# Short-tile combination on GpSimd and strip copy on VectorE in an attention and mixture-of-experts block

## What is computed

```python
q, k, v = x @ wq.T, x @ wk.T, x @ wv.T          # 8 heads, 2 maps of 32, v of 32
scores = einsum('bhqd,bhkd->bhqk', q, k) / sqrt(dh)      # 16 maps, causal
attn = softmax(scores + causal, axis=-1)
attn = attn[:, :8] - attn[:, 8:] * lmbda                 # the two maps of a head
out = einsum('bhqk,bhkd->bhqd', attn, v)
o = out * rsqrt(mean(out ** 2 over groups of 4) + eps) * (1 - L_INIT)
x = x + (o @ wo.T) * silu(ffn(layernorm(x)))
```

## Time and profile before

| | us |
|---|---|
| median of 3 runs | 1129.12 (1128.27 to 1133.16) |
| the profiled execution | 1129.73 |
| its span | 1127.9 |

### The profile page before, as it was taken

How to read it: one execution, slowest core, us unless ns; L and a number is a source line. 1 busy time by engine, 2 the same in 40 slices (tenths; PEclk the granted TensorE clock), 3 DMA queues, 4 the chain that set the end, 5 groups by cost and what they waited for, 6 DMA issues and landing times. The chain is left out here.

```text
span 1127.9 us, 25764 instructions
## 1 busy us (share of the span) xinstructions
PE 945.8 (84%) x6626; PEld 662.2 (59%) x6627; DVE 937.6 (83%) x1873; ACT 776.0 (69%) x1982; POOL 222.6 (20%) x427
## 2 busy tenths in 40 slices
PE   5889875899999899898998988967999999963665
PEld 4777653666666666666666666644555555532544
DVE  6677667999999999999999999954777777754886
ACT  3544245999999999999999999962333333325563
POOL 2000000132222222222222222220000000017771
PEclk9999985999999999999999999998999999986677
DMA  7999965768777686775756657401222222223563
GB/s 260 353 359 335 330 258 146 160 163 202 171 173 165 158 204 170 178 160 117 165 128 137 155 119 166 99 20 59 79 80 84 79 79 83 79 92 95 168 184 104
DMA packets 92410, 178.11 MB, mean 158 GB/s; under 512 B 11744, under 2 KB 50144, under 8 KB 91360
## 3 DMA queue, kind: packets, MB, share of 16 engines
q1 hardware_dynamic: 74336, 147.38, 48.9%
q0 software_dynamic: 7680, 20.98, 6.5%
q10 hardware_dynamic: 10368, 9.44, 2.5%
HBM read 108.56 MB, written 69.21 MB: 158 GB/s over the span
## 5 line engine op out<-in xcount | busy, mean ns | idle before, releaser
L1049 DVE TENSOR_REDUCE nmax<-bank 128x1 f32<-128x1024 f32 (+3 forms) x256 | 259.8, 1015 | 4.2 <-PE bank L881 4.1
L982 ACT ACTIVATE Pr_long<-bank,nmax 128x1024 f32<-128x1024 f32 (+3 forms) x256 | 252.1, 985 | 11.0 <-DVE nmax L1049 10.8
L1009 ACT COPY AT<-bank 128x512 f32<-128x512 f32 (+3 forms) x384 | 177.1, 493 | 3.8 <-PE bank L920 1.8
L879 PE MATMUL bank<-Ks_first,Qs_first 128*128 128x512 f32 (+3 forms) x384 | 124.2, 413 | 31.1 <-ACT Pr_short L996 19.8
L996 ACT ACTIVATE Pr_short<-bank,nmax 128x128 f32<-128x128 f32 (+3 forms) x256 | 138.4, 541 | 8.9 <-DVE nmax L1067 1.7
L1241 PE MATMUL bank<-gu_sb,xsT 128*128 x288 | 139.8, 609 | 4.7 <-DVE hid L1358 0.5
L920 PE MATMUL bank<-ident,Pr_long 128*128 128x128 f32 x832 | 127.4, 280 | 18.1 <-DVE Pr_long L1099 18.0
L1099 DVE SCALAR_TENSOR_TENSOR Pr_long<-Pr_long,coef 128x1024 f32<-128x1024 f32 (+3 forms) x128 | 137.3, 1073 | 0.0
L879 PE MATMUL bank<-Ks_second,Qs_second 128*128 128x512 f32 (+3 forms) x384 | 119.4, 400 | 18.4 <-ACT Pr_short L996 18.1
L881 PE MATMUL bank<-maskb,identb 128*128 128x128 bf16 x512 | 118.1, 233 | 0.0
L920 PEld LDWEIGHTS bank<-ident,Pr_long 128*128 128x128 f32 x832 | 90.4, 142 | 31.4 <-issue 27.3
(11 more groups left out here) (147 smaller groups left out, 1634.5 us busy)
## 6 DMA issues: line engine op xcount, KB each, us to landing
q_parts<-PARTS SPq DMA_DIRECT2D x32, 512.0 KB, 5.1
k_parts<-PARTS SPq DMA_DIRECT2D x32, 512.0 KB, 3.7
Qs_first<-q_parts SPq DMA_DIRECT2D x64, 256.0 KB
Ks_first<-k_parts SPq DMA_DIRECT2D x64, 256.0 KB
Qs_second<-q_parts SPq DMA_DIRECT2D x64, 256.0 KB, 6.1
Ks_second<-k_parts SPq DMA_DIRECT2D x64, 256.0 KB, 7.0
xs_dram<-zeros SPq DMA_DIRECT2D x8, 1152.0 KB, 7.4
xs<-xs_dram SPq DMA_DIRECT2D x72, 128.0 KB, 2.0
```

The lines of the kernel that those rows point to most:

```text
L879: nc.tensor.matmul(at[:, c0:c1], Qs[head][:, m, q * P:(q + 1) * P], Ks[head][:, m, c0:c1], start=True, stop=(c1 < N))
L982: nc.scalar.activation(long_probs(p)[:, m, 0:N], long_slot[m][:, 0:N], ACT.Exp, bias=nmax[:, 4 * p + m:4 * p + m + 1], scale=1.0, accum_ou ...
L1009: nc.scalar.copy(AT[u % 6][:, 0:w], tb[u % BANKS][:, 0:w]).then_inc(unit_out, 1)
L1049: nc.vector.tensor_reduce(nmax[:, 4 * p + m:4 * p + m + 1], long_slot[m][:, 0:N], AX.X, ALU.max, negate=True).then_inc(long_maxed, 1)
```

## The change

`combine_short` moves from VectorE to GpSimd, where it is two instructions: the second map is scaled in place by `coef`, and behind a wait on its own semaphore (`short_scaled`) it is added to the first. `out_rows` moves from ScalarE to VectorE, with the last copy behind the loop. The frames of all engines are written anew; GpSimd's program is now run by `run_pairs` with a lead of four, with the two copies of V as steps of pairs 1 and `NP` - 3. The diff, without its semaphore declarations:

```diff
             short_slot = bank[2][:, 0:CH]
@@ -801,6 +803,22 @@
                         for u in range(2):
                             load(it + 1, u)
 
+                def combine_short(it, p):
+
+                    if absent(it, p):
+                        return
+                    it, p = place(it, p)
+                    N = (short_q(p) + 1) * P
+                    probs = short_probs(p)
+                    nc.gpsimd.wait_ge(coef_done, credited(it, NP, p))
+
+                    nc.gpsimd.sem_inc(combine_begun, 1)
+                    nc.gpsimd.tensor_scalar(probs[:, 1, 0:N], probs[:, 1, 0:N], coef[:, 2 * p:2 * p + 1], None, ALU.mult
+                                            ).then_inc(short_scaled, 1)
+                    nc.gpsimd.wait_ge(short_scaled, credited(it, NP, p))
+                    nc.gpsimd.tensor_tensor(probs[:, 0, 0:N], probs[:, 1, 0:N], probs[:, 0, 0:N], ALU.add
+                                            ).then_inc(short_combined, 1)
+
                 @block.gpsimd
                 def _(pool):
                     pool.sem_inc(vj_ready, 2)
@@ -850,26 +868,33 @@
                         nc.gpsimd.tensor_copy(d1_all[:, bass.ds(it * 2 + u, 1), :],
                                               dsum[u][:, :, 0].unsqueeze(1)).then_inc(d1_kept, 1)
 
-                    def iteration(it):
-                        for p in range(NP):
+                    def frame(it, p):
+                        if p >= 0:
                             if p == 0:
                                 for u in range(2):
-                                    copy_v(it, u)
                                     load_rows(it, u)
                             keep_rows(it, p)
-                            if p in SORT_AT:
-                                sort_rows(it, *SORT_AT[p])
-                            if p == 2:
-                                keep_d1(it, 0)
-                        keep_d1(it, 1)
-                        for u in range(2):
-
-                            pool.wait_ge(rows_sorted[u], 32 * (it + 1))
+                            if p == 1 and not (isinstance(it, int) and it == 0):
+                                copy_v(it, 1)
+                            if p == NP - 3 and not (isinstance(it, int) and it == NIT - 1):
+                                copy_v(it + 1, 0)
+                        combine_short(it, p + 4)
+                        if p in SORT_AT:
+                            sort_rows(it, *SORT_AT[p])
+                        if p == 2:
+                            keep_d1(it, 0)
+                        if p == NP - 1:
+                            keep_d1(it, 1)
+                            for u in range(2):
+
+                                pool.wait_ge(rows_sorted[u], 32 * (it + 1))
 
                     pool.sem_inc(o_kept, NP)
-                    iteration(0)
-                    with pool.Fori(1, NIT) as it:
-                        iteration(it)
+                    pool.sem_inc(short_combined, NP)
+                    pool.sem_inc(short_scaled, NP)
+                    for u in range(2):
+                        copy_v(0, u)
+                    run_pairs(pool, 4, frame)
                     keep_rows(NIT - 1, NP)
 
                 def score_into(at, head, q, m):
@@ -954,16 +979,16 @@
                     pe.sem_inc(pv_done, NP)
 
                     def frame(it, p):
+                        score_short(it, p + 2, 1)
+                        score_long(it, p + 3, 0)
+                        turn(it, p, LONG1)
                         turn(it, p + 1, LONG0)
                         score_short(it, p + 3, 0)
                         score_long(it, p + 3, 1)
                         turn(it, p + 1, SHORT)
                         values(it, p)
-                        score_short(it, p + 3, 1)
-                        score_long(it, p + 4, 0)
-                        turn(it, p + 1, LONG1)
-
-                    run_pairs(pe, 4, frame)
+
+                    run_pairs(pe, 3, frame)
                     pe.wait_ge(o_out, credited(NIT - 1, NP, NP - 1))
                     sum_rows(NP - 1).then_inc(pv_done, 1)
 
@@ -1008,36 +1033,22 @@
                     w = len(unit_blocks(p, k)) * P
                     nc.scalar.copy(AT[u % 6][:, 0:w], tb[u % BANKS][:, 0:w]).then_inc(unit_out, 1)
 
-                def out_rows(it, p):
-
-                    if absent(it, p):
-                        return
-                    it, p = place(it, p)
-                    nc.scalar.wait_ge(pv_done, credited(it, NP, p))
-                    nc.scalar.wait_ge(o_kept, credited(it, NP, p - 2))
-                    nc.scalar.copy(Ob[p % 2][:], ob[:, 0:P + 2 * DH]).then_inc(o_out, 1)
-
                 @block.scalar
                 def _(act):
                     act.sem_inc(long_exped, 2 * NP)
                     act.sem_inc(short_exped, 2 * NP)
                     act.sem_inc(unit_out, UNITS)
-                    act.sem_inc(o_out, NP)
 
                     def frame(it, p):
-                        exp_long(it, p + 3, 1)
-                        out_rows(it, p)
-                        exp_short(it, p + 3, 1)
-                        turn_out(it, p + 1, LONG1)
-                        turn_out(it, p + 2, LONG0)
-                        exp_long(it, p + 4, 0)
-                        exp_short(it, p + 4, 0)
-                        turn_out(it, p + 2, SHORT)
-
-                    run_pairs(act, 4, frame)
-                    act.wait_ge(pv_done, credited(NIT - 1, NP, NP))
-                    act.wait_ge(o_kept, credited(NIT - 1, NP, NP - 2))
-                    nc.scalar.copy(Ob[0][:, P:], ob[:, P:P + 2 * DH]).then_inc(o_out, 1)
+                        exp_long(it, p + 2, 1)
+                        exp_short(it, p + 2, 1)
+                        turn_out(it, p, LONG1)
+                        exp_long(it, p + 3, 0)
+                        exp_short(it, p + 3, 0)
+                        turn_out(it, p + 1, LONG0)
+                        turn_out(it, p + 1, SHORT)
+
+                    run_pairs(act, 3, frame)
 
                 def max_long(it, p, m):
 
@@ -1100,17 +1111,14 @@
                         out=probs[:, 0, 0:N], in0=probs[:, 1, 0:N], scalar=coef[:, 2 * p + 1:2 * p + 2],
                         in1=probs[:, 0, 0:N], op0=ALU.mult, op1=ALU.add).then_inc(long_combined, 1)
 
-                def combine_short(it, p):
+                def out_rows(it, p):
 
                     if absent(it, p):
                         return
                     it, p = place(it, p)
-                    N = (short_q(p) + 1) * P
-                    probs = short_probs(p)
-                    nc.vector.wait_ge(coef_done, credited(it, NP, p))
-                    nc.vector.scalar_tensor_tensor(
-                        out=probs[:, 0, 0:N], in0=probs[:, 1, 0:N], scalar=coef[:, 2 * p:2 * p + 1],
-                        in1=probs[:, 0, 0:N], op0=ALU.mult, op1=ALU.add).then_inc(short_combined, 1)
+                    nc.vector.wait_ge(pv_done, credited(it, NP, p))
+                    nc.vector.wait_ge(o_kept, credited(it, NP, p - 2))
+                    nc.vector.tensor_copy(Ob[p % 2][:], ob[:, 0:P + 2 * DH]).then_inc(o_out, 1)
 
                 @block.vector
                 def _(dve):
@@ -1119,19 +1127,22 @@
                     dve.sem_inc(rec_done, NP)
                     dve.sem_inc(coef_done, NP)
                     dve.sem_inc(long_combined, NP)
-                    dve.sem_inc(short_combined, NP)
+                    dve.sem_inc(o_out, NP)
 
                     def frame(it, p):
-                        max_short(it, p + 1, 1)
-                        max_long(it, p + 2, 0)
-                        inverse(it, p + 1)
-                        combine_short(it, p)
-                        ratio(it, p + 1)
-                        max_short(it, p + 2, 0)
-                        max_long(it, p + 2, 1)
-                        combine_long(it, p + 1)
-
-                    run_pairs(dve, 2, frame)
+                        max_short(it, p + 3, 0)
+                        max_long(it, p + 3, 1)
+                        combine_long(it, p + 2)
+                        max_short(it, p + 3, 1)
+                        max_long(it, p + 4, 0)
+                        inverse(it, p + 3)
+                        out_rows(it, p)
+                        ratio(it, p + 3)
+
+                    run_pairs(dve, 4, frame)
+                    dve.wait_ge(pv_done, credited(NIT - 1, NP, NP))
+                    dve.wait_ge(o_kept, credited(NIT - 1, NP, NP - 2))
+                    nc.vector.tensor_copy(Ob[0][:, P:], ob[:, P:P + 2 * DH]).then_inc(o_out, 1)
 
 
         with ExitStack() as ph:
```

More of the change, by code:

```diff
@@ L743, in build @@
             keep_begun = sem("keep_begun")
+            combine_begun = sem("combine_begun")
+            short_scaled = sem("short_scaled")
             long_slot = [bank[0], bank[1]]
```

## The result

The changed kernel takes 1238.84 us (median of 4 runs, 1238.02 to 1239.65), the one before 1128.69 in the same comparison: a ratio of 1.097, interval 1.0951 to 1.099. It is 110 us slower, where 1150 us and at most 1172 had been forecast: the direction was right, the size was off by a factor of five.

The account below looks back on a forecast made before the run. VectorE was taken to set the pace. Its relief net of waits, -16.6 us, and stalls behind GpSimd's sum, +37.1, gave +20.5 on the profiled 1129.73 us: 1150 us, with a range from 1113 to 1172.

Parts of the forecast that it names:

- The queue behind GpSimd's wait: On GpSimd: only `keep_rows` and TensorE's short transposes queue there; the transposes start 4.65 us behind `ratio`, GpSimd done at 2.55.
- renumbering: In all engines' frames: other reordering, lead-in and run-out, costed at nothing; ScalarE's listed `turn_out` move got no cost either.
- The third rival: GpSimd becomes the bound: its queue slips over 2 us, TensorE waits for short transposes; adds 32 us, 1182; chance 0.06.
- The exclusion: VectorE's `combine_long` waits while GpSimd sums: stalls of 1.16 us per four pairs, 37.1 us in the stage.
- A to D: Pairs with short tiles of 128, 256, 384, 512 keys (long 1024, 896, 768, 640); stalls 0, 0.14, 0.51, 0.51 us.
- the sign of being right: `combine_long` of C and D recorded 1.5 and 1.4 us instead of 1.00 and 0.87, those of A unchanged.
- The failed term: GpSimd's scaling of the second map, taken as 0.39, 0.50, 0.60, 0.71 us for A to D.
- The sum's price: GpSimd's sum of two maps at 2.5 passes, 2.08 ns an element: 0.45, 0.72, 0.99, 1.25 us.
- the rule that the wait is the overlap less 0.20 us: GpSimd lets VectorE go ahead of its recorded end, so 0.20 us came off each stall; without it, 1169 us.
- VectorE's relief: Per four pairs on VectorE: short combinations of 1.81 us gone, strip copies of 1.08 added, 0.73 saved.
- the waits that follow: VectorE, coming earlier, waits for TensorE at the long maximum: 0.24 us in A, 0.16 in B, none in C, D.
- VectorE sets the pace: In the attention stage VectorE's steps nearly all follow directly, ScalarE has room; four pairs take 17.70 us.

Follow-up runs that it names:

- 3: no scaling: experiment 1 with GpSimd's scaling and the wait behind it taken out, only the sum left there: 1126.13 us, ratio 0.996 to the kernel before.
- 6: ScalarE's order: The kernel before with only ScalarE's `turn_out` of LONG0 moved behind `exp_long(..,0)` and `exp_short(..,0)`: 1151.54 us, ratio 1.0198.
- 7: sum behind: experiment 1 with GpSimd's sum also waiting for `combine_long` of its pair: 1129.32 us, ratio 0.9993 to the kernel before.
- 8: both: experiment 7 with ScalarE's `turn_out` of LONG0 back ahead of the exponentials: 1118.21 us, ratio 0.9893 to the kernel before.
- experiment 1: The changed kernel with both `keep_d1` steps put ahead of `combine_short` on GpSimd: 1145.13 us, ratio 1.0148 to the kernel before.
- 2: The changed kernel with only the `keep_d1` of frame 7 put ahead of `combine_short`, that of frame 2 left behind it: 1153.5 us.
- experiment 5: The changed kernel with `combine_short` kept on VectorE behind `out_rows`, none on GpSimd, and `keep_d1` as in experiment 1: 1161.5 us, ratio 1.0283 to the kernel before.
- 4: experiment 1 with `out_rows` left on ScalarE and ScalarE's order as before: 1148.06 us, ratio 1.0166 to the kernel before.
- 9: experiment 7 with `out_rows` and ScalarE's order as in the kernel before: 1125.64 us, ratio 0.9966 to the kernel before.

## Why the prediction was wrong

**What VectorE waits for, step by step.** I took the mean of each step on VectorE (start to start, 250 to 640 us of the timelines) in five kernels. A four, in us; steps that are equal in all are left out.

| step, summed over a four | before | 3: no scaling | 6: ScalarE's order | 7: sum behind | 8: both |
|---|---|---|---|---|---|
| `combine_short` or `out_rows` | 1.84 | 1.08 | 1.85 | 1.09 | 1.06 |
| `inverse` to its follower, four times | 0.34 | 0.42 | 0.38 | 0.42 | 0.38 |
| maximum 768 to `inverse` | 0.87 | 1.05 | 1.31 | 1.05 | 0.87 |
| maximum 896 to `inverse` | 1.22 | 1.20 | 1.27 | 1.20 | 1.02 |
| maximum 1024 to `inverse` | 1.13 | 1.13 | 1.20 | 1.13 | 1.13 |
| `ratio` to the short maximum, four times | 0.60 | 0.93 | 0.64 | 1.00 | 0.98 |
| short maximum of A to maximum 1024 | 0.33 | 0.52 | 0.40 | 0.52 | 0.52 |
| `combine_long` 768 and 896 | 1.99 | 1.99 | 1.99 | 1.99 | 2.10 |
| sum | 8.32 | 8.33 | 9.03 | 8.40 | 8.06 |
| difference x 32 | | 0 | +23 | +3 | -8 |
| measured difference | | -4 | +21 | -1 | -12 |

The differences of the sums follow the measured ones within 4 us, and always lie above them. From the first `ratio` to the last the stage takes 553.5, 554.2, 575.0, 555.5 and 546.4 us in these five, which agrees with the sums. So the 4 us gained without the scaling, and some of the 12 of experiment 8, lie outside the stage's steps; where is open.

**The queue behind GpSimd's wait: the step that failed.** The prediction said: "Queued behind GpSimd's new wait are `keep_rows` (its buffer is wanted two pairs later) and TensorE's short transposes". It left out `keep_d1`, and with it the one waiter that had no slack, ScalarE's `exp_long` of a head's first pair. Experiments 1 and 2 put 94 us on it. I had read the new frame for what it adds and called the rest renumbering at a cost of nothing, but a step that stands for p + 4 had come in front of one that stands for p. The third rival had the form of this failure (GpSimd's queue slips and another engine waits) and the wrong waiter; it was priced at 1182 us and given 0.06.

**The exclusion: right in kind, wrong in place.** I forecast stalls of 0, 0.14, 0.51 and 0.51 us in A to D, and named `combine_long` of C and D, 0.5 us longer, as the sign of being right. In the changed kernel B has 0.49 in mean and C and D next to none (1.040 and 0.876 us over the stage). In experiment 1, in mean, A has 0.11 (0.23 in every second one), B 0.47, C 0.04 and D none: 0.62 a four or 20 us, where I had 1.16 and 37. Experiments 3 and 7 remove it, for 19 and 16 us. The failed term is the scaling, 0.60 to 1.56 us where the trace's one small tensor_scalar had led me to 0.39 to 0.71: at 32 elements it couldn't show a slope, and I had put all that it takes beyond a copy into the fixed part. It moved the sum in C and D behind the start of `combine_long`, so that GpSimd waits there, which costs nothing (in experiment 7 it waits longer, and the kernel gets faster). The sum's price, 2.5 passes, was right (2.15 ns an element between 128 and 256 keys, and the Trainium skill's figure of 4497 ns for 2048 elements, GPSIMD Engine Reference, section Performance versus the Vector engine, comes to an estimated 2.2). The same page says in its section When to use GPSIMD that one-input operations run at about line rate. The copy's 0.83 ns an element fits that; the scaling doesn't, at 2.5, and the measurement decides. Right too was the rule that the wait is the overlap less 0.20 us: in B the sum ends 0.70 us behind the start of `combine_long`, and this is delayed by 0.51. The Trainium skill (SBUF — State Buffer, Terms) would have it wait the whole 0.70; the trace doesn't agree by 0.19.

**VectorE's relief: right by itself, but its successor was mis-sized.** Going from 1.84 to 1.06 is 0.78, where I had 0.73. Of the waits that follow I forecast 0.40. Experiment 8 has 0.24 ahead of the two maxima of A (forecast 0.24) and 0.22 ahead of the short maximum of B (forecast 0.16, at its long one). Where I had none it has 0.12 ahead of the short maxima of C and D, 0.11 at `combine_long` and 0.04 behind `inverse`: 0.73 in all. ScalarE's shorter chain gives 0.20 at the 896 maximum there, as forecast (0.19).

**ScalarE's order: not costed.** "All else is renumbering ... which I cost at nothing" covered the move of `turn_out` behind the two exponentials as well. It costs 21 us alone (experiment 6) and 11 us in the changed kernel (8 against 7), and it hid the 0.20 us at the 896 maximum. I had even listed the move, and had not looked for who waits behind it.

**What bounds the kernel.** "VectorE sets the pace" holds for added work (experiment 5), but taking work away is worth a fraction (4, 8 and 9). A chain stands right behind it: short maximum, short exponential, the next scores, long maximum (the lines of experiment 8). The earlier trace rows had shown its lag of 0.06 us in one place, and I used it in two places only.

The account of the 110 us: +94 `keep_d1`, +16 the exclusion, +11 ScalarE's order, and -12 for the two moves themselves. These are the differences along one chain of kernels (changed, experiments 1, 7, 8, before), so they add up of themselves and hold in this order only: ScalarE's order, taken alone in the kernel before, costs 21. The forecast of 1150 us lies near the 1145 of experiment 1 by luck: the stall is half as large (16 to 19 us instead of 37), the relief 12 instead of 17, and 11 us of ScalarE's order, forecast at nothing, stand beside them.

## What to carry to other kernels

When a step is put into an in-order queue, list every instruction that now stands behind it, the shortest too, and ask for each who waits for it and when; a copy of 0.18 us behind 3.3 us of new work cost 94 us over 16 iterations, while the exclusion that I had worked out to tenths of a microsecond cost 16 to 19. Number the steps by absolute iteration when frames are shifted: a step for p + 4 ahead of one for p makes the old depend on the new. An engine without gaps in the trace sets the price of added work, not the gain from removed work; for this, look how close behind it the next chain runs, at every shape.

## What the runs showed of the hardware

- GpSimd's tensor_scalar on float32 takes 0.28 us and 2.5 ns an element (0.603 us at 128, 1.564 at 512), three times its copy's 0.83 ns; with a constant factor 0.550 and 1.499. Its two-input sum, undisturbed, takes 2.15 ns an element (0.455 at 128, 0.730 at 256). The scaling with one input is dearer than the sum with two.
- VectorE's `combine_long` and GpSimd's sum exclude each other, and a lead of 0.03 us is enough: in B GpSimd had the lead and VectorE lost 0.51 us, in C VectorE had it (at times by 0.05 us only) and GpSimd lost the time. `combine_long`, where it loses, waits for what is left of the sum, less 0.16 to 0.20 us. A wait that fixes the turn (experiment 7) was worth 16 us.
- GpSimd's indirect DMAs, 1.03 us before, take 1.245 in mean in the changed kernel, and 1.75 at 512.80, where one started while `combine_long` (511.93 to 513.58) was running. Those that start just ahead of a `combine_long` keep 1.05 (0.13 us ahead, in the same trace). It cost nothing that the runs show.
